# Layer-norm centring moved from ScalarE to VectorE in a strided view, and the score masking moved ahead of the reciprocal

## The chip, the cores and the metric

The kernel runs on one core of a Trainium2 chip. The metric is the time of one execution on the device in microseconds (us), taken as the median of several runs. Lower is better. The engines are TensorE (PE in the profile; PEld is its weight load), VectorE (DVE), ScalarE (ACT), GpSimd (POOL) and SyncE (SP), which issues the DMAs.

## The reference, cut to what matters

One transformer layer over x of 16 batches x 512 tokens x 128 channels, in two parts.

```
mod = (silu(c) @ wmod).reshape(16, 6, 1, 128);  sa, ca, ga, sb, cb, gb = ...
h = layernorm(x) * (1 + ca) + sa                 # centring: (x - mean) / sqrt(var + eps)
x = x + ga * attn(h)                             # rms_norm, q/k/v for 16 heads of 64, rope,
                                                 # softmax in a causal window of 32, w_out
h = layernorm(x) * (1 + cb) + sb
x = x + gb * ffn(h)                              # small attention, layer norm, 8 experts by argmax, layer norm
```

Only the first part, the attention, is touched.

## The kernel before, in words

The attention part is one loop, written out in full, over steps `s` = 0 to 136. There are 16 batches and 8 steps for each (`G = 8`), since a step takes two of the 16 heads; `b, r = s // 8 + 1, s % 8`, so that within a step `r` is the place in the batch and `b` the next batch. Each engine has its own list of instructions, in the order in which the code is written, and semaphores join the lists. Nothing is reordered by a scheduler: an instruction that waits holds everything behind it on its engine.

A pair of heads passes through a pipeline of steps, so that in one step each engine works on several pairs:

- step s: TensorE projects q and k of pair s (lines 323 to 325, three matmuls each for a high/low split), VectorE multiplies them by cos and sin (L503, L504, four instructions, `mm`), SyncE issues four DMAs that swap halves (`sw<-mm`, L222) and three for the values (`vw<-vn`).
- step s+1: GpSimd adds the two halves (L621, `qk`).
- step s+2 (`LS`): TensorE forms the scores (L337). VectorE adds the mask and takes the minimum in eight instructions (L528, `sm` and `mn`), the **masking**.
- step s+3 (`LE`): ScalarE takes the exponential (L692, eight instructions, `pr` and `sums`). VectorE takes the **reciprocal** of the sums (L511, `ri`). GpSimd **normalises** with it (L627, `pr<-pr,ri`).
- step s+4: TensorE transposes `pr` (L352), ScalarE copies it to `pT` (L702). Step s+5: TensorE multiplies by the values (L368), ScalarE and VectorE split the result in a high and a low part (L711 `oth`, L548 `otl`).
- step s+6: TensorE accumulates the output projection of the batch in one PSUM bank, `ACC` (L393, L394, L396). When the eighth pair of a batch is in, VectorE copies `ACC` to `yt` (L518). This is in a step with r = 6. The next batch's first accumulation, also in a step with r = 6, may not start before that copy is done: TensorE waits on `s_yt` ahead of L393.

Beside it the next batch's input is prepared, a little in each step. VectorE takes the statistics of x in a step with r = 3 (`layer_stats`, L412, L417). GpSimd forms 1/sqrt(var + eps) at r = 7 (`shape`, L569, L571, `lnr`) and, for ScalarE's form of the centring, -mean times it (L572, L574, `lnb`). ScalarE **centres** in two halves at r = 0 and r = 1, as its last work of the step (L673, four instructions of 128 x 128 for each batch, `hh`). GpSimd multiplies `hh` by the modulation at r = 1 (L578) and adds at r = 2 (L582), ScalarE squares at r = 3 and 4 (L654), GpSimd finishes the rms norm at r = 4 and 5. At r = 6 TensorE transposes the result (L288), ScalarE copies it (L661, `xh`), and VectorE forms its low part (L428, `xl`, the function `x_low`), for which the q projection of the next step (r = 7) waits, since both use the same PSUM banks in turn.

VectorE's order within a step is: rope (L503, L504), reciprocal, copy of `yt` (r = 6 only), masking, `x_low` (r = 6 only), the gated output (L541, r = 0 only), `otl`, statistics (r = 3 only). The first batch is centred on VectorE ahead of the loop (L422).

Of the kernel before, what the change touches and what calls it, by code (L numbers as in the profile page):

```python
# [10 lines left out]
ALU = mybir.AluOpType  # L11
ACT = mybir.ActivationFunctionType
AX = mybir.AxisListType

P = 128
NB, T, C = 16, 512, 128
NH, G = 16, 8
NI = NB * G
# [8 lines left out]
WK, NW = 96, T // 64  # L27


def program(nc, a, out, debug=None):  # L30
# [7 lines left out]
    with top:  # L38
        def sbt(ctx, name, shape, dt=F32):
            return ctx.enter_context(nc.sbuf_tensor(name, shape, dt))  # L40
# [19 lines left out]
        p1 = ExitStack()  # L60
# [14 lines left out]
        lnr = sbt(p1, "lnr", [P, 4])  # L75
        lnb = sbt(p1, "lnb", [P, 4])
        ssq = sbt(p1, "ssq", [P, 4])
# [53 lines left out]
        s_mk = sem("a_mk")  # L131
# [53 lines left out]
        with nc.Block(no_gpsimd_drain=True) as blk:  # L185
# [214 lines left out]
            def _(dve):  # L400
# [18 lines left out]
                def centre(b):  # L419
                    dve.wait_ge(s_ln, 4 * b + 2)  # L420
                    for j in range(4):
                        ins = dve.tensor_scalar(hh[:, j, :], xt[b % 4][:, j, :], mv[:, j, 0:1], lnr[:, j:j + 1],  # L422
                                                ALU.subtract, ALU.mult)
                    ins.then_inc(s_hc, 1)
# [68 lines left out]
                for s in range(SLOTS):  # L493
                    for j in range(2):
                        if s < NI:
                            u = pj_use[("rope", s, j)]
                            dve.wait_ge(s_pj, u + 1)
                            if s == 0:
                                dve.wait_ge(s_cs, 32)
                            if s >= 2 and j == 0:  # L500
                                dve.wait_ge(s_add, s - 1)
                                dve.wait_ge(s_sw[s % 2], 64 * (s // 2))
                            dve.tensor_tensor(mm[s % 2][:, 0, j, :], PJ[u % 2][:, :], cos[:, :], ALU.mult)  # L503
                            dve.tensor_tensor(mm[s % 2][:, 1, j, :], PJ[u % 2][:, :], sin[:, :], ALU.mult)\  # L504
                                .then_inc(s_rope, 1)
                    i = s - LE
                    if 0 <= i < NI:
# [5 lines left out]
                    if 0 <= i < NI and i % G == G - 1:  # L513
# [4 lines left out]
                        dve.tensor_copy(yt[:, :], ACC[:, :]).then_inc(s_yt, 1)  # L518
                    i = s - LS
                    if 0 <= i < NI:  # L520
                        dve.wait_ge(s_sc, i + 1)
                        if i == 0:
                            dve.wait_ge(s_mk, 3)
                        if i >= 2:
                            dve.wait_ge(s_exp, 2 * i - 2)
                        for h in range(2):
                            for p in range(4):
                                ins = dve.tensor_tensor_reduce(ms_[i % 2][:, h, p, :], SC[h][:, p * WK:(p + 1) * WK],  # L528
                                                               msk[:, min(p, 1), :], 1.0, 3.0e38, ALU.add, ALU.min,
                                                               mn[i % 2][:, h, p:p + 1])  # L530
                            ins.then_inc(s_mx, 1)
                    if s % G == 6 and s // G + 1 < NB:
# [17 lines left out]
                    if s in (2, 3):  # L550
# [3 lines left out]
                                          woh[:, 4 * m:4 * m + 4, :].bitcast(F32), ALU.subtract).then_inc(s_wol, 1)  # L554
                    if s % G == 3 and s // G + 2 < NB:
                        layer_stats(s // G + 2)

            @blk.gpsimd
            def _(pool):
# [4 lines left out]
                def shape(b):  # L564
# [4 lines left out]
                    pool.tensor_scalar(lnr[:, :], mv[:, :, 1], EPS, None, ALU.add).then_inc(s_ln, 1)  # L569
                    pool.wait_ge(s_ln, 4 * b + 1)  # L570
                    pool.tensor_tensor(lnr[:, :], lnr[:, :], nhalf[:, :], ALU.pow).then_inc(s_ln, 1)  # L571
                    pool.tensor_scalar(lnb[:, :], mv[:, :, 0], -1.0, None, ALU.mult).then_inc(s_ln, 1)  # L572
                    pool.wait_ge(s_ln, 4 * b + 3)
                    pool.tensor_tensor(lnb[:, :], lnb[:, :], lnr[:, :], ALU.mult).then_inc(s_ln, 1)  # L574
                    yield
# [72 lines left out]
            def _(act):  # L648
# [16 lines left out]
                for n in range(3):  # L665
                    c = slice(1024 * n, 1024 * n + 1024)
                    act.wait_ge(s_wf[n], 16)
                    act.activation(wh[:, c], wf3[:, c], ACT.Copy, scale=(-0.125, 1.0, 1.0)[n]).then_inc(s_whi, 1)
                def centre(b, k):
                    act.wait_ge(s_ln, 4 * b + 4)  # L670
                    act.wait_ge(s_xn, b)
                    for j in (2 * k, 2 * k + 1):
                        ins = act.activation(hh[:, j, :], xt[b % 4][:, j, :], ACT.Identity, scale=lnr[:, j:j + 1],  # L673
                                             bias=lnb[:, j:j + 1])
                    if k:
                        ins.then_inc(s_hc, 1)

                act.wait_ge(s_rm, 2)
# [4 lines left out]
                for s in range(SLOTS):  # L683
# [33 lines left out]
                    if s < NI:  # L717
# [6 lines left out]
                        act.activation(vn[s % 4][:, :], PJ[u % 2][:, :], ACT.Copy).then_inc(s_ve, 1)  # L724
                    if b < NB and r in (0, 1):
                        centre(b, r)
                    if b < NB and r in (3, 4):
# [860 lines left out]
```

## Time and profile before

| | |
|---|---|
| median of 3 runs | 1189.38 us (1188.65 to 1190.33) |
| the profiled execution's own time | 1190.33 us |
| its span in the trace | 1188.4 us |
| PE busy | 1066.2 us, 90% |
| DVE busy | 940.7 us, 79% |
| ACT busy | 923.1 us, 78% |
| POOL busy | 874.5 us, 74% |
| L673, the centring on ACT, x60 | 26.1 us busy |
| L511, the reciprocal, x128 | 25.2 us busy, 27.0 us idle before it, 26.4 of them for ACT pr |
| L528, the masking, x1024 | 189.8 us busy |

The busy times overlap: all engines work at once, and the shares say nothing yet of which one sets the pace. A row of the timeline gives the start, the length, the engine, the line and what was computed; idle time of the engine just before the row stands in brackets with what ended it. Instructions of one engine overlap by some tens of nanoseconds, so the distance between two starts is the cost of the first, and the length printed is a little more. The attention part lasts until about 775 us; what follows it is not touched.

### The profile page before, as it was taken

How to read it: one execution, taken by the hardware profiler on the slowest of the kernel's cores; microseconds unless marked ns; L12 is line 12 of the kernel's file. 1: busy time of each engine (PE TensorE's matmuls, PEld its weight loads, DVE VectorE, ACT ScalarE, POOL GpSimd, SP SyncE). 2: the span in 40 equal slices, each digit the busy share in tenths (PEclk: the TensorE clock that was granted, in tenths of full speed). 3: DMA queues.
4: the chain of work that ended last, by engine and by line, in shares of the span. 5: the costliest groups of instructions: out<-in, count | busy, mean ns of one | idle time of the engine just before them, and what ended most of it. 6: DMA issues, size and time to landing. Idle time of an engine off the chain costs nothing. (4 is left out here: it accounts for less than half of the span.)

```text
span 1188.4 us, 51662 instructions
## 1 busy us (share of the span) xinstructions
PE 1066.2 (90%) x18513; PEld 863.6 (73%) x18513; DVE 940.7 (79%) x4130; ACT 923.1 (78%) x3404; POOL 874.5 (74%) x732
## 2 busy tenths in 40 slices
PE   4799999999999999999999998847998884499994
PEld 2577877777778777877877886635877774488883
DVE  6988988889889889889888886446887864288885
ACT  2799999999999999999999996736866752266662
POOL 2788888888888888888878875454666767167777
PEclk7999999999999999999999998859998885699997
DMA  6777777776776777777776776262243122666210
GB/s 199 197 183 170 189 180 170 187 182 166 194 178 167 191 177 174 186 178 171 187 177 167 179 180 152 71 196 73 66 140 106 56 81 106 196 194 178 85 33 31
DMA packets 111036, 181.02 MB, mean 152 GB/s; under 512 B 19726, under 2 KB 64177, under 8 KB 110656
## 3 DMA queue, kind: packets, MB, share of 16 engines
q1 hardware_dynamic: 102944, 158.53, 52.5%
q0 software_dynamic: 6400, 16.82, 3.9%
q8 instruction: 152, 2.49, 0.9%
q10 hardware_dynamic: 1440, 2.36, 0.7%
q14 instruction: 100, 0.82, 0.2%
HBM read 35.20 MB, written 24.73 MB: 50 GB/s over the span
## 5 line engine op out<-in xcount | busy, mean ns | idle before, releaser
L621 POOL TENSOR_TENSOR qk<-mm,sw 128x1024 f32<-128x1024 f32 x128 | 305.1, 2384 | 115.3 <-DMA sw<-mm 114.8
L692 ACT ACTIVATE pr<-sm,mn 128x96 f32<-128x96 f32 x1024 | 368.5, 369 | 0.3 <-DVE mn L528 0.3
L503 DVE TENSOR_TENSOR mm<-bank,cos 128x512 f32<-128x512 f32 x256 | 175.1, 684 | 70.9 <-PE bank L325 58.9
L692 ACT ACTIVATION_READ_ACCUMULATOR pr<-sm,mn 128x1 f32 x1024 | 200.8, 196 | 0.0
L627 POOL TENSOR_TENSOR pr<-pr,ri 128x768 f32<-128x768 f32 x128 | 188.8, 1475 | 3.4 <-DVE ri L511 3.4
L528 DVE CUSTOM_DVE_ANT_0 sm<-bank,msk 128x96 f32<-128x96 f32 x1024 | 189.8, 250 | 0.0
L504 DVE TENSOR_TENSOR mm<-bank,sin 128x512 f32<-128x512 f32 x256 | 174.0, 680 | 0.0
L368 PE MATMUL bank<-pT,vw 96*64 96x64 f32 x4096 | 150.3, 227 | 0.0
L702 ACT ACTIVATE pT<-bank 96x512 f32<-96x512 f32 x256 | 137.0, 585 | 17.1 <-PE bank L352 15.3
L368 PEld LDWEIGHTS bank<-pT,vw 96*64 96x64 f32 x4096 | 132.5, 140 | 10.4 <-issue 0.7
L337 PEld LDWEIGHTS bank<-qk 64*64 64x64 f32 x4096 | 90.7, 133 | 55.9 <-issue 54.4
L337 PE MATMUL bank<-qk 64*64 64x96 f32 x4096 | 114.7, 250 | 9.3 <-POOL qk L621 9.3
L1295 ACT ACTIVATE fv<-bank,b1t 128x128 f32<-128x128 f32 x288 | 82.4, 369 | 52.1 <-PE bank L1156 51.9
L323 PE MATMUL bank<-xh,wh 128*128 128x512 f32 x256 | 104.9, 410 | 3.3 <-DVE xl L428 1.4
L724 ACT ACTIVATE vn<-bank 128x512 f32<-128x512 f32 x128 | 76.2, 596 | 37.4 <-PE bank L301 37.3
L325 PE MATMUL bank<-xh,wl 128*128 128x512 f32 x256 | 102.4, 400 | 0.0
L324 PE MATMUL bank<-xl,wh 128*128 128x512 f32 x256 | 101.9, 398 | 0.0
L1002 POOL DMA_INDIRECT out<-h,rr x72 | 76.7, 1065 | 30.5 <-issue 27.0
L548 DVE TENSOR_TENSOR otl<-bank,oth 128x512 fp32r<-128x512 f32 x128 | 87.7, 685 | 8.4 <-ACT oth L711 8.4
L352 PE MATMUL bank<-ident,pr 64*96 64x64 f32 x2048 | 84.0, 222 | 6.2 <-POOL pr L627 5.9
L997 POOL DMA_INDIRECT sorted_scratch<-rr,slot x64 | 65.6, 1025 | 29.2 <-issue 17.9
L528 DVE DVE_READ_ACCUMULATOR2_ANT mn<- 128x1 f32 x1024 | 84.5, 83 | 0.1
(210 smaller groups left out, 2476.8 us busy)
## 6 DMA issues: line engine op xcount, KB each, us to landing
sw<-mm SPq DMA_DIRECT2D x512, 128.0 KB, 2.4
vw<-vn SPq DMA_DIRECT2D x128, 192.0 KB, 2.6
vw<-vn SPq DMA_DIRECT2D x128, 128.0 KB, 2.4
rr<-sorted_scratch SPq DMA_DIRECT2D x72, 192.5 KB, 2.7
vw<-vn SPq DMA_DIRECT2D x96, 64.0 KB, 2.2
xt<-in_x SPq DMA_DIRECT2D x16, 256.0 KB, 4.5
x_scratch<-x SPq DMA_DIRECT2D x16, 256.0 KB, 2.7
rr<-x_scratch SPq DMA_DIRECT2D x16, 256.0 KB, 2.9
```

The source lines that it names most:

```text
L323: pe.matmul(dst[:, :], wh[:, o:o + P], xh[b % 2][:, :], start=True, stop=False)
L324: pe.matmul(dst[:, :], wh[:, o:o + P], xl[b % 2][:, :], start=False, stop=False)
L325: pe.matmul(dst[:, :], wl[:, o:o + P], xh[b % 2][:, :], start=False, stop=True).then_inc(s_pj, 1)
L337: ins = pe.matmul(SC[h][64 * e:64 * e + 64, p * WK:(p + 1) * WK], t[r, 0, 32 + 64 * w:96 + 64 * w], t[r, 1, 64 * w:64 * w + WK], start=Tru ...
L368: ins = pe.matmul(OB[64 * h:64 * h + 64, 64 * w:64 * w + 64], vw[half % 2][:, w, c:c + 64], pT[i % 2][:, h, 64 * w:64 * w + 64], start=Tru ...
L503: dve.tensor_tensor(mm[s % 2][:, 0, j, :], PJ[u % 2][:, :], cos[:, :], ALU.mult)
L504: dve.tensor_tensor(mm[s % 2][:, 1, j, :], PJ[u % 2][:, :], sin[:, :], ALU.mult)\
L528: ins = dve.tensor_tensor_reduce(ms_[i % 2][:, h, p, :], SC[h][:, p * WK:(p + 1) * WK], msk[:, min(p, 1), :], 1.0, 3.0e38, ALU.add, ALU.mi ...
L621: pool.tensor_tensor(qk[i % 2][:, :, 32:], mm[i % 2][:, 0, :, :], sw[i % 2][:, :, :], ALU.add)\
L627: pool.tensor_tensor(t, t, ri[i % 2][:, :].unsqueeze(2).to_broadcast([P, 8, WK]), ALU.mult)\
L692: ins = act.activation(pr[i % 2][:, h, p, :], ms_[i % 2][:, h, p, :], ACT.Exp, scale=-1.0, bias=mn[i % 2][:, h, p:p + 1], accum_out=sums[i ...
L702: act.activation(pT[i % 2][:, :, :].rearrange("k h (p e q) -> k (h p) e q", p=4, e=2)[:, :, e, :], TR[e][0:WK, :].rearrange("k (a q) -> k ...
```

## The change: what it does

1. The centring of batches 1 to 15 leaves ScalarE and enters VectorE's list at r = 1, behind `otl`, all four instructions in one step. It waits for `lnr`, and for the previous batch's `xn`.
2. The centring on VectorE, the first batch's too, reads and writes its 128 elements in the order 0, 2, 4, ..., 126, 1, 3, ..., 127: a view of 2 x 64 with a step of 2 elements inside.
3. GpSimd no longer forms `lnb` (two instructions for each batch), and the counts of its semaphore are adjusted.
4. In VectorE's list the masking of pair s-2 now comes straight behind the rope, ahead of the reciprocal of pair s-3 and of the copy of `yt`.

```diff
@@ centre, now for all batches @@
-                    dve.wait_ge(s_ln, 4 * b + 2)
+                    dve.wait_ge(s_ln, 2 * b + 2)
+                    if b:
+                        dve.wait_ge(s_xn, b)
                     for j in range(4):
-                        ins = dve.tensor_scalar(hh[:, j, :], xt[b % 4][:, j, :], mv[:, j, 0:1], lnr[:, j:j + 1],
-                                                ALU.subtract, ALU.mult)
+                        o, x = (v.rearrange("p (a k) -> p k a", k=2) for v in (hh[:, j, :], xt[b % 4][:, j, :]))
+                        ins = dve.tensor_scalar(o, x, mv[:, j, 0:1], lnr[:, j:j + 1], ALU.subtract, ALU.mult)
                     ins.then_inc(s_hc, 1)
@@ VectorE's loop: the masking block moves up unchanged, from behind the yt copy @@
+                    i = s - LS
+                    if 0 <= i < NI:
+                        dve.wait_ge(s_sc, i + 1)
...
+                            ins.then_inc(s_mx, 1)
                     i = s - LE
                     if 0 <= i < NI:
                         dve.wait_ge(s_exp, 2 * i + 2)
@@ end of VectorE's loop @@
-                    if s % G == 3 and s // G + 2 < NB:
-                        layer_stats(s // G + 2)
+                    b, r = s // G + 1, s % G
+                    if b < NB:
+                        if r == 1:
+                            centre(b)
+                    if r == 3 and b + 1 < NB:
+                        layer_stats(b + 1)
@@ GpSimd, shape @@
-                    pool.tensor_scalar(lnb[:, :], mv[:, :, 0], -1.0, None, ALU.mult).then_inc(s_ln, 1)
-                    pool.wait_ge(s_ln, 4 * b + 3)
-                    pool.tensor_tensor(lnb[:, :], lnb[:, :], lnr[:, :], ALU.mult).then_inc(s_ln, 1)
@@ ScalarE @@
-                def centre(b, k):
-                    act.wait_ge(s_ln, 4 * b + 4)
-                    act.wait_ge(s_xn, b)
-                    for j in (2 * k, 2 * k + 1):
-                        ins = act.activation(hh[:, j, :], xt[b % 4][:, j, :], ACT.Identity, scale=lnr[:, j:j + 1],
-                                             bias=lnb[:, j:j + 1])
-                    if k:
-                        ins.then_inc(s_hc, 1)
...
-                    if b < NB and r in (0, 1):
-                        centre(b, r)
```

VectorE's list in a step with r = 6, before; L528 is the masking (each instruction has a second row for its minimum), and the names in brackets are the semaphores waited for:

```order
L504 TENSOR_TENSOR mm<-bank,sin 128x512
L511 RECIPROCAL ri<-sums 128x8 [waits a_nm,a_exp]
L518 COPY yt<-bank 128x512 [waits a_pj,a_op]
L528 ISA sm,mn<-bank,msk 128x96 [waits a_exp,a_sc]
L528 ISA mn 128x1
...
L428 TENSOR_TENSOR xl<-bank,xh 128x512 [waits a_xh]
```

And the same step now, where the lines have moved (L516 is the masking, L525 the reciprocal, L532 the copy of `yt`, L429 the low part of x):

```order
L505 TENSOR_TENSOR mm<-bank,sin 128x512
L516 ISA sm,mn<-bank,msk 128x96 [waits a_exp,a_sc]
L516 ISA mn 128x1
...
L525 RECIPROCAL ri<-sums 128x8 [waits a_nm,a_exp]
L532 COPY yt<-bank 128x512 [waits a_pj,a_op]
L429 TENSOR_TENSOR xl<-bank,xh 128x512 [waits a_xh]
```

The eight masking instructions now stand between the last rope instruction and both the reciprocal and the copy; the low part of x has the same instructions ahead of it as before.

VectorE's list at the end of a step with r = 1 now, the next step's rope behind it; before, L548 (`otl`) was followed at once by the rope:

```order
L525 RECIPROCAL ri<-sums 128x8 [waits a_nm,a_exp]
L549 TENSOR_TENSOR otl<-bank,oth 128x512 [waits a_op,a_ot]
L424 TENSOR_SCALAR hh<-xt,mv,lnr 128x2x64 [waits a_xn,a_ln]
L424 TENSOR_SCALAR hh<-xt,mv,lnr 128x2x64 x3
L504 TENSOR_TENSOR mm<-bank,cos 128x512 [waits a_sw0,a_add,a_pj]
```

Four instructions (L424) have come in ahead of the next step's rope.

## Rows read from the trace of the kernel before

**Rows 1.** By stretch: length, busy PE, PEld, DVE, ACT, POOL; clock, DMA share, GB/s.
```profile
70.00:704.00 634.00, 630.40 (x10449) 504.93 (x10446) 561.41 (x2629) 601.92 (x2429) 536.12 (x365) 1.00 0.72 178
```

**Rows 2.** Waits over the whole run: us in total, times, longest.
```profile
DVE ri L511 <- ACT pr L692: 26.4, 56, 3.0
...
PEld bank L323 <- DVE xl L428: 9.8, 16, 1.8
```

**Rows 3.** Timeline of DVE, step 70 (r = 6): start, length, engine, line.
```profile
415.90 0.69 DVE L503 TENSOR_TENSOR mm<-bank,cos 128x512 f32<-128x512 f32 x1 [0.35 <-PE bank L325]
...
418.31 0.19 DVE L511 RECIPROCAL ri<-sums 128x8 f32<-128x8 f32 x1
418.42 0.64 DVE L518 COPY yt<-bank 128x512 f32<-128x512 f32 x1
...
420.39 0.68 DVE L428 TENSOR_TENSOR xl<-bank,xh 128x512 fp32r<-128x512 f32 x1
```

**Rows 4.** Timeline of PE at the same place, steps 70 and 71.
```profile
420.17 0.39 PE L393 MATMUL bank<-oth,woh 128*128 128x512 f32 x1
420.40 0.39 PE L394 MATMUL bank<-oth,wol 128*128 128x512 f32 x1
...
421.13 0.50 PE L323 MATMUL bank<-xh,wh 128*128 128x512 f32 x1
421.47 0.39 PE L324 MATMUL bank<-xl,wh 128*128 128x512 f32 x1
```

**Rows 5.** Timeline of PE and DVE, step 126 (the last with r = 6).
```profile
743.02 0.39 PE L393 MATMUL bank<-oth,woh 128*128 128x512 f32 x1
...
741.54 0.19 DVE L511 RECIPROCAL ri<-sums 128x8 f32<-128x8 f32 x1
```

**Rows 6.** Timeline of ACT at the end of the loop (steps 127, 128).
```profile
748.68 0.60 ACT L724 ACTIVATE vn<-bank 128x512 f32<-128x512 f32 x1 [0.28 <-PE bank L301]
749.17 0.37 ACT L692 ACTIVATE pr<-sm,mn 128x96 f32<-128x96 f32 x1
```

**Rows 7.** Timeline of DVE, step 65 (r = 1) into step 66.
```profile
391.20 0.20 DVE L511 RECIPROCAL ri<-sums 128x8 f32<-128x8 f32 x1 [0.39 <-ACT pr L692]
391.32 0.26 DVE L528 CUSTOM_DVE_ANT_0 sm<-bank,msk 128x96 f32<-128x96 f32 x1
...
392.75 0.69 DVE L548 TENSOR_TENSOR otl<-bank,oth 128x512 fp32r<-128x512 f32 x1
393.79 0.69 DVE L503 TENSOR_TENSOR mm<-bank,cos 128x512 f32<-128x512 f32 x1 [0.36 <-PE bank L325]
```

**Rows 8.** Timeline of POOL, steps 65 and 66.
```profile
392.02 1.48 POOL L627 TENSOR_TENSOR pr<-pr,ri 128x768 f32<-128x768 f32 x1
394.00 1.28 POOL L578 TENSOR_TENSOR hh<-hh,mod 128x512 f32<-128x512 f32 x1 [0.50 <-ACT hh L673]
397.01 2.42 POOL L621 TENSOR_TENSOR qk<-mm,sw 128x1024 f32<-128x1024 f32 x1 [1.73 <-DMA sw<-mm]
399.38 1.48 POOL L627 TENSOR_TENSOR pr<-pr,ri 128x768 f32<-128x768 f32 x1
```

**Rows 9.** Timeline of PE, step 67 (r = 3).
```profile
400.91 0.65 PE L352 MATMUL bank<-ident,pr 64*96 64x64 f32 x16 [0.18 <-POOL pr L627]
```

**Rows 10.** Timeline of DVE and POOL, step 2.
```profile
35.08 2.10 DVE L553 TENSOR_TENSOR wol<-x,woh 128x512 fp32r<-128x512 f32 x1
...
34.26 2.38 POOL L621 TENSOR_TENSOR qk<-mm,sw 128x1024 f32<-128x1024 f32 x1 [1.86 <-DMA sw<-mm]
```

**Rows 11.** The line of the first batch's centring: ns min/median/max, first and last start.
```profile
L422 DVE TENSOR_SCALAR hh<-xt,mv,lnr x4: 345/346/348, 6.5 to 7.3; 128x128 f32<-128x128 f32 x4
```

**Rows 12.** Timeline of POOL, steps 7 to 8 (first batch), and PE behind it.
```profile
70.41 0.23 POOL L572 TENSOR_SCALAR lnb<-mv 128x4 f32<-128x4 f32 x1
...
70.88 2.41 POOL L621 TENSOR_TENSOR qk<-mm,sw 128x1024 f32<-128x1024 f32 x1
...
74.77 0.65 PE L352 MATMUL bank<-ident,pr 64*96 64x64 f32 x16 [0.29 <-POOL pr L627]
```

More of the change, by code:

```diff
@@ L75, in program @@
         lnr = sbt(p1, "lnr", [P, 4])
-        lnb = sbt(p1, "lnb", [P, 4])
         ssq = sbt(p1, "ssq", [P, 4])
@@ L505, in _ @@
                                 .then_inc(s_rope, 1)
+                    i = s - LS
+                    if 0 <= i < NI:
+                        dve.wait_ge(s_sc, i + 1)
+                        if i == 0:
+                            dve.wait_ge(s_mk, 3)
+                        if i >= 2:
+                            dve.wait_ge(s_exp, 2 * i - 2)
+                        for h in range(2):
+                            for p in range(4):
+                                ins = dve.tensor_tensor_reduce(ms_[i % 2][:, h, p, :], SC[h][:, p * WK:(p + 1) * WK],
+                                                               msk[:, min(p, 1), :], 1.0, 3.0e38, ALU.add, ALU.min,
+                                                               mn[i % 2][:, h, p:p + 1])
+                            ins.then_inc(s_mx, 1)
                     i = s - LE
@@ L518, in _ @@
                         dve.tensor_copy(yt[:, :], ACC[:, :]).then_inc(s_yt, 1)
[L519 to L531, printed above, removed]
                     if s % G == 6 and s // G + 1 < NB:
@@ L569, in shape @@
                     pool.tensor_scalar(lnr[:, :], mv[:, :, 1], EPS, None, ALU.add).then_inc(s_ln, 1)
-                    pool.wait_ge(s_ln, 4 * b + 1)
+                    pool.wait_ge(s_ln, 2 * b + 1)
                     pool.tensor_tensor(lnr[:, :], lnr[:, :], nhalf[:, :], ALU.pow).then_inc(s_ln, 1)
-                    pool.tensor_scalar(lnb[:, :], mv[:, :, 0], -1.0, None, ALU.mult).then_inc(s_ln, 1)
-                    pool.wait_ge(s_ln, 4 * b + 3)
-                    pool.tensor_tensor(lnb[:, :], lnb[:, :], lnr[:, :], ALU.mult).then_inc(s_ln, 1)
                     yield
```

## The prediction, on record before the changed kernel was run

> **What bounds the kernel now.** I read the busy time by stretch first. From 70 to 704 us TensorE is busy 630.4 of 634 us at full granted clock [rows 1]. ScalarE with 601.9 and VectorE with 561.4 are nearly full beside it, but not full. TensorE is one nearly unbroken row of matmuls, 3.6 us of idle in 634. So in this stretch a change pays or costs only where TensorE waits. Second I read the waits. VectorE's reciprocal waits 26.4 us in total for ScalarE [rows 2], which looks large, but it is idle time of an engine that TensorE paces: the rope behind it waits for TensorE in every step shown [rows 3, 7]. TensorE's own repeated wait is one at r = 7, where L323 waits for `xl`: 9.8 us over 16 batches as its weight load sees it [rows 2]. Third I read the timeline around each place where the change moves something, and asked which TensorE instruction waits for it and how much room it has.
>
> **The order on VectorE, r = 6: the copy of `yt`.** Eight masking instructions take 392.75 - 391.32 = 1.43 us [rows 7]. They now stand ahead of the reciprocal (0.11 us to the next start) and the copy. The copy therefore starts at 418.31 + 1.43 + 0.11 = 419.85 instead of 418.42 [rows 3]. L393 of the next batch waits for its end. How long after its start can TensorE go on? The low part of x, as long (0.68 against 0.64), starts at 420.39 and TensorE starts at 421.13, 0.74 later [rows 3, 4]; less 0.04 for the shorter instruction that is 0.70. So L393 starts at about 420.55 instead of 420.17 [rows 4]: a new wait of 0.38 us. But TensorE was about to wait there anyway. Before, L393, L394 and L396 were done in time and L323 then waited until 421.13. Now they run at 420.55, 420.89 (the first matmul after a wait is followed after 0.34 us, 421.47 - 421.13, and not after 0.23, 420.40 - 420.17 [rows 4]) and 421.12, and L323 comes at 421.35. `xl` itself is not later, since the same instructions stand ahead of it and their sum is the same. L324 comes at 421.58 instead of 421.47: 0.11 us for each batch. There are 15 steps with r = 6 at which a copy and a waiting L393 meet, s = 14 to 126. For 14 of them this holds: 14 x 0.11 = 1.5 us. The last one, s = 126, has no next batch and no `xl` to hide behind. There the copy would start at 741.54 + 1.54 = 743.08 and L393 at 743.78 instead of 743.02 [rows 5], with 0.11 for the restart: 0.87 us. Does the end of the loop hide it? ScalarE takes pair 125's exponentials at 749.17 straight behind the values of step 127, which wait for TensorE [rows 6], with no idle between. If ScalarE or anything later had slack there, it would cost 0; I find no such slack in these rows and count it in full. Sum of this edit: 2.4 us slower.
>
> **The order on VectorE, every step: the masking earlier, the reciprocal later.** The masking no longer stands behind the wait of 0.39 us [rows 7], so it gains 0.4 to 0.5 us in such steps. No TensorE wait for it is worth a row, so nothing comes of it in time. The reciprocal is 1.43 us later where it did not wait, about 1.0 us where it did. It releases the normalising on GpSimd (L627). Where GpSimd comes to it later anyway, as at 399.38 behind the addition that waited 1.73 us for a DMA [rows 8], nothing is lost. At r = 1 it moves from 392.02 to about 390.73 (rope ended) + 1.43 + 0.28 = 392.4, with the transposes three microseconds off. I take 0 here, except as in the next part.
>
> **The centring on VectorE, r = 1.** ScalarE loses 26.1 us of work (the table), VectorE gains 60 instructions. The contiguous form takes 345 ns each and starts every 0.26 us ((7.3 - 6.5)/3) [rows 11]; the strided form is not in the trace. Lower bound 4 x 0.26 = 1.0 us for a batch, upper bound 4 x 0.346 = 1.4 us, as if nothing overlapped; I take 1.0, nearest to the row. Can GpSimd hold it up? L553, an instruction of VectorE on two SBUF operands, took 2.10 us against 0.69 for `otl` of the same size, and ended half a microsecond after GpSimd's L621 ended (34.26 + 2.38 = 36.64) [rows 7, 10]: it waited out the whole GpSimd instruction. The centring has one tensor operand. If it waits in the same way, it stands behind the normalising, which now runs from 392.4 to 393.9; if not, it starts at 392.9 behind `otl`. So the rope of step 66 starts at 393.9 + 1.0 = 394.9 or at 393.9, against 393.79 [rows 7]: 0.1 to 1.1 us later, and with the upper bound of the centring up to 1.5. The Trainium skill, in "SBUF — State Buffer", section "Who interferes with whom", says that tensor_scalar in a two-port mode takes the pair of ports that VectorE shares with GpSimd, for the whole instruction. In "VectorE: DVE Perf Modes", section "Mode 2×_2P", it makes that mode depend on an even outermost dimension, which the 2 of the new view is as well. By that rule the later start, 394.9, holds in either view; I take it.
>
> Who waits for that rope? The next reciprocal no longer waits in front of the masking, so half of the delay is taken back. Masking starts at 394.9 + 2.41 = 397.3 (four rope instructions, 418.31 - 415.90 [rows 3]) and the reciprocal at 398.7. Normalising is possible from 399.0. GpSimd was at it at 399.38 in this batch, where the addition waits for its DMA; in batches whose DMA is earlier the new bound is 399.0, end 400.5. TensorE's transposes would come at 400.91 - 0.18 = 400.73 [rows 9]. So 0.2 us of room is left. Behind the rope stand the step's DMAs on SP and the addition of step 67 on GpSimd, which itself stands behind the 1.3 us of L582 (as long as L578 [rows 8]), so it could start no earlier than 399.38 + 1.48 + 1.28 = 402.1. The step's four DMAs have from 397.3 until then, 4.8 us; the step before's took from about 391 to 397.01 with a transfer queued ahead. If they should need as much, the addition is 1 us late, and the room of the transposes behind it decides; I count 0. The multiplication L578 starts at 395.1 instead of 394.0 and ends at 396.4, ahead of 397.01 [rows 8]. Cost 0; if the room is missed, see B.
>
> **GpSimd without `lnb`, r = 7.** 0.47 us less for a batch (70.88 - 70.41) [rows 12]. In a steady batch the next addition waits for its DMA and nothing comes of it. In the first batch the addition follows at once and TensorE waits 0.29 us for what follows: 0.3 us faster, once. ScalarE's freed time, 26.1 us, lies off TensorE's path: 0. The startup (steps 0 to 3) is paced by the DMA queue (the addition there waits 1.86 us for it [rows 10]), and a late centring there costs at most 1 us, by its 4 x 0.26; I take 0.
>
> **The sum**, on the profiled execution's 1190.33 us (span 1188.4): + 1.5 + 0.9 - 0.3 = + 2.1, so 1192.4. The profiled execution is the slowest of the three; their median is 0.95 lower, so 1191.5 us for the median.
>
> **Rivals.** A is the sum above. **B, slower:** the normalising misses the transposes at r = 3. It decides from the 0.2 us of room: with a strided centring of 0.346 us each, 0.35 more, TensorE waits 0.15 in each of 15 batches; with half a microsecond more lost at the hand-over it waits 0.65. That is 2 to 10 us on top of A; I price it at 5: 1196.5. For it speaks that such a wait is there already in some batches [rows 9], against it that the late ones come from the DMA and would hide the centring. **C, faster:** ScalarE was the true pace, since its 601.9 of 634 us leave little room [rows 1]. Then up to 26.1 us come back: 1163, or 1189.4 - 26.1/2 = 1176 if every second batch gains. Against it: the row of matmuls has no gap for ScalarE to have made. **D, no change:** the waits for `yt` are taken up by the loop's other slack (an earlier DMA against the later TensorE), 1189.4.
>
> **Numbers.** A 0.58, B 0.15, C 0.07, D 0.20. A measurement of this kernel can tell about 0.2%, 2.4 us, so slower begins at 1191.8. A's own range is 1190.2 to 1193; four tenths of it lie beyond 1191.8. Slower: 0.24 + 0.15 = 0.39. Faster: 0.07 + 0.02 of D = 0.09. Same: 0.52. The range for eight in ten takes in D and most of B: 1188.6 to 1197.
>
> **What would show it.** PE L393 waits at r = 6, 0.3 to 0.4 us, for the copy of `yt`, and the `xl` wait of the next matmul is gone or short. At s = 126 that wait is 0.75 us. The rope of a step with r = 2 starts up to 1.1 us later and the reciprocal's wait for ScalarE is nearly gone from the list, with the time unmoved. The centring's first instruction is longer than the other three if GpSimd holds it. ScalarE is 26 us less busy. The prediction is wrong if TensorE's steps with r = 1 to 3 grow (B), or if steps that had no wait become shorter (C).

## The result, and the profile after

The changed kernel takes 1195.54 us (median of 20 runs, 1189.73 to 1203.61) beside 1189.09 us of the kernel before on the same chip (20 runs, 1179.77 to 1194.13). The ratio is 1.006, 95% interval 1.0043 to 1.0078: slower by 0.4 to 0.8%. The predicted 1191.5 us had the direction of case A, to which the prediction gave 0.58, but by its own limit of 0.2% it held "same" for likelier (0.52) than "slower" (0.39). The measured time lies in its range, near the upper end, and the addition of 6.5 us is three times the 2.1 us that the sum gave. Each ratio in this text is worked out from the fast runs of both kernels, so it is not always the quotient of the two medians beside it.

The profiled execution took 1199.29 us with a span of 1197.4. That is 3.8 us above the median of its kernel, and the profiled execution of before is 1.2 above its own, so the two traces lie 9.0 us apart and the medians 6.5. The attention stretch first: length, busy PE, PEld, DVE, ACT, POOL; clock, DMA share, GB/s.

```profile
70.00:704.00 634.00, 623.83 (x10323) 498.29 (x10323) 575.22 (x2650) 583.83 (x2347) 525.17 (x332) 1.00 0.70 176
```

TensorE was busy 630.4 us in this stretch [rows 1] and is busy 623.8 now, and 126 fewer of its matmuls fall into it. ScalarE is busy 18 us less and VectorE 14 us more, at the same granted clock (over the whole run ScalarE fell by 12 us, from 923.1 to 910.9, where the prediction said 26). Freed time on ScalarE bought nothing. What TensorE lost can be read from its waits in the same stretch, of the kernel after (total us, times, longest):

```profile
PE bank L392 <- DVE yt L532: 4.0, 14, 0.3
PE bank L351 <- POOL pr L629: 3.8, 10, 0.4
PE bank L336 <- POOL qk L623: 2.3, 5, 1.2
```

And of the kernel before:

```profile
PE bank L352 <- POOL pr L627: 1.5, 5, 0.4
PE bank L337 <- POOL qk L621: 0.5, 1, 0.5
```

The wait for the copy of `yt` is new. The waits for GpSimd, for the normalising and for the addition, were there and have grown from 2.0 us in 6 places to 6.1 in 15. I measured each step as the distance from the first value matmul of the step before to its own (L299 before, L298 after). From step 8 to step 120 the sum went from 631.3 to 639.5 us. Of these 8.2 us, 14 steps with r = 7 hold 2.2 (5.82 to 5.98 each), 14 with r = 3 hold 2.4 (5.64 to 5.81), 14 with r = 4 hold 2.7 (5.47 to 5.66); the rest is scattered. The step s = 127 adds 0.9, and step 8 is reached 0.8 us earlier.

**The copy of `yt`.** PE and DVE at r = 6, step 70, of the kernel after:

```profile
424.31 0.64 DVE L532 COPY yt<-bank 128x512 f32<-128x512 f32 x1
425.09 0.47 PE L392 MATMUL bank<-oth,woh 128*128 128x512 f32 x1 [0.29 <-DVE yt L532]
425.40 0.39 PE L393 MATMUL bank<-oth,wol 128*128 128x512 f32 x1
425.63 0.40 PE L395 MATMUL bank<-otl,woh 128*128 128x512 f32 x1
425.87 0.40 PE L322 MATMUL bank<-xh,wh 128*128 128x512 f32 x1
426.10 0.39 PE L323 MATMUL bank<-xl,wh 128*128 128x512 f32 x1
```

The wait sits where the prediction put it, and L322 follows L395 after 0.24 us with no wait for `xl` any more. L392 starts 0.78 us behind the start of the copy (the prediction took 0.70). At the last such step, s = 126:

```profile
750.55 0.64 DVE L532 COPY yt<-bank 128x512 f32<-128x512 f32 x1
751.34 0.47 PE L392 MATMUL bank<-oth,woh 128*128 128x512 f32 x1 [0.67 <-DVE yt L532]
```

The same matmul started at 743.02 [rows 5], so 8.3 us are gathered by here, of the 9.0 by which the two spans differ.

**The centring.** DVE from step 17 (r = 1) into step 18, of the kernel after:

```profile
122.34 1.93 DVE L424 TENSOR_SCALAR hh<-xt,mv,lnr 128x128 f32<-128x128 f32 x4
124.19 0.68 DVE L504 TENSOR_TENSOR mm<-bank,cos 128x512 f32<-128x512 f32 x1
```

Four instructions of 0.34 us, which start every 0.26, would be over in 1.1 us. They take 1.93. GpSimd in the same kernel at the same time, and on into step 19:

```profile
121.95 1.47 POOL L629 TENSOR_TENSOR pr<-pr,ri 128x768 f32<-128x768 f32 x1 [0.69 <-DVE ri L525]
124.42 1.28 POOL L580 TENSOR_TENSOR hh<-hh,mod 128x512 f32<-128x512 f32 x1 [1.00 <-DVE hh L424]
126.11 2.41 POOL L623 TENSOR_TENSOR qk<-mm,sw 128x1024 f32<-128x1024 f32 x1 [0.42 <-DMA sw<-mm]
...
132.64 2.41 POOL L623 TENSOR_TENSOR qk<-mm,sw 128x1024 f32<-128x1024 f32 x1 [1.45 <-DMA sw<-mm]
```

The normalise, released by the late reciprocal, runs from 121.95 to 123.42, and the first centring instruction, 1.16 us long by itself, is over 0.08 us behind it. So it is in 14 of the 15 batches: the first centring instruction ends 0.08 or 0.09 us behind a GpSimd instruction that was running. The rope L504 starts at 124.19, straight behind the centring. Before, the rope waited for TensorE instead:

```profile
123.30 0.39 PE L325 MATMUL bank<-xh,wl 128*128 128x512 f32 x1
123.73 0.69 DVE L503 TENSOR_TENSOR mm<-bank,cos 128x512 f32<-128x512 f32 x1 [0.35 <-PE bank L325]
```

The same matmul in the kernel after:

```profile
122.91 0.40 PE L324 MATMUL bank<-xh,wl 128*128 128x512 f32 x1
```

So the rope is 1.28 us behind its matmul and not 0.43: 0.85 us late, and 0.93 on average over the 14 steps with r = 2 from 9 to 119 (measured from the first value matmul of the step before). The rope's DMAs are late with it, by 0.81 us on average. DMA issues of SP in this place, of the kernel after:

```profile
126.69 2.65 SPq L221 DMA_DIRECT2D sw<-mm  x4
```

and of the kernel before, with the addition that followed:

```profile
126.24 2.65 SPq L222 DMA_DIRECT2D sw<-mm  x4
...
131.27 2.40 POOL L621 TENSOR_TENSOR qk<-mm,sw 128x1024 f32<-128x1024 f32 x1
```

Before, the addition came 5.0 us behind the start of the issues and did not wait for them. After, it came 5.95 us behind and waited 1.45. So the DMAs were issued late and were also slow here. TensorE, at step 20 (r = 4), of the kernel after:

```profile
135.20 0.89 PE L336 MATMUL bank<-qk 64*64 64x96 f32 x32 [0.24 <-POOL qk L623]
136.54 0.65 PE L351 MATMUL bank<-ident,pr 64*96 64x64 f32 x16 [0.45 <-POOL pr L629]
```

The transposes' wait (L351) has the same cause: their normalising (L629) starts straight behind the late addition. So it is in all ten of L351's waits in this stretch: the normalising starts straight behind an addition that had waited for its DMA, and never behind the late reciprocal.

**Which of these waits can come from the late rope.** The rope that stands behind the centring is that of a step with r = 2. Its addition is in the next step and its scores are in the one after, r = 4. So through its own DMAs and addition the late rope reaches TensorE at r = 4, not at r = 3. Of the 6.1 us of waits for GpSimd, 2.1 are at r = 4, where before had none, and 3.8 at r = 3, where before had 1.7 of its 2.0 (the rest stands at other steps). The waits at r = 3 stand behind DMAs of the steps with r = 1, which are issued ahead of the centring. The longest of all is one of them, in steps 65 to 67 of the kernel after:

```profile
391.19 0.69 DVE L504 TENSOR_TENSOR mm<-bank,cos 128x512 f32<-128x512 f32 x1 [0.70 <-PE bank L324]
394.82 2.42 SPq L221 DMA_DIRECT2D sw<-mm  x4
395.68 2.26 DVE L424 TENSOR_SCALAR hh<-xt,mv,lnr 128x128 f32<-128x128 f32 x4
401.46 2.39 POOL L623 TENSOR_TENSOR qk<-mm,sw 128x1024 f32<-128x1024 f32 x1 [2.11 <-DMA sw<-mm]
404.00 0.89 PE L336 MATMUL bank<-qk 64*64 64x96 f32 x32 [1.18 <-POOL qk L623]
```

The rope is over and the four issues are under way before the centring starts, and the addition still waits for them, until 6.6 us behind the first issue. From the first of the four issues to the last landing it took, at r = 1, 4.3 to 6.1 us in the trace of before and 4.3 to 6.6 in that of after; at r = 2 it took 4.1 to 5.6 and 4.1 to 5.9.

**The late reciprocal.** GpSimd's wait for it, from the page of the kernel after, in the columns busy, mean ns, idle before and releaser:

```profile
L629 POOL TENSOR_TENSOR pr<-pr,ri 128x768 f32<-128x768 f32 x128 | 188.6, 1473 | 35.1 <-DVE ri L525 34.2
```

and of the kernel before:

```profile
L627 POOL TENSOR_TENSOR pr<-pr,ri 128x768 f32<-128x768 f32 x128 | 188.8, 1475 | 3.4 <-DVE ri L511 3.4
```

The 26.4 us of VectorE's wait for ScalarE [rows 2] are gone from the page, and GpSimd has 31 us of new idle time in their place. The experiments ask which of these is paid for.

### The profile page after: what moved, and what is told of

It is laid out like the page before. It is cut to its first block and busy times, and to the rows that moved or that the text cites. A ratio compares the mean times of both kernels' runs of the same rounds, so it can differ in the third digit from the quotient of the medians.

```text
span 1197.4 us, 51615 instructions
## 1 busy us (share of the span) xinstructions
PE 1067.7 (89%) x18513; PEld 863.6 (72%) x18513; DVE 963.9 (81%) x4190; ACT 910.9 (76%) x3344; POOL 869.2 (73%) x700
## 5 line engine op out<-in xcount | busy, mean ns | idle before, releaser
L504 DVE TENSOR_TENSOR mm<-bank,cos 128x512 f32<-128x512 f32 x256 | 175.1, 684 | 72.8 <-PE bank L324 62.1
L629 POOL TENSOR_TENSOR pr<-pr,ri 128x768 f32<-128x768 f32 x128 | 188.6, 1473 | 35.1 <-DVE ri L525 34.2
L685 ACT ACTIVATION_READ_ACCUMULATOR pr<-sm,mn 128x1 f32 x1024 | 195.9, 191 | 0.0
L516 DVE CUSTOM_DVE_ANT_0 sm<-bank,msk 128x96 f32<-128x96 f32 x1024 | 191.0, 252 | 3.0 <-PE bank L336 3.0
L322 PE MATMUL bank<-xh,wh 128*128 128x512 f32 x256 | 103.5, 404 | 2.7 <-DVE xl L429 1.4
L323 PE MATMUL bank<-xl,wh 128*128 128x512 f32 x256 | 102.1, 399 | 0.0
L549 DVE TENSOR_TENSOR otl<-bank,oth 128x512 fp32r<-128x512 f32 x128 | 84.7, 662 | 14.6 <-ACT oth L704 14.0
L351 PE MATMUL bank<-ident,pr 64*96 64x64 f32 x2048 | 85.0, 224 | 5.7 <-POOL pr L629 5.5
L516 DVE DVE_READ_ACCUMULATOR2_ANT mn<- 128x1 f32 x1024 | 84.6, 83 | 0.0
```

What stands on the lines that cost most here:

```text
L322: pe.matmul(dst[:, :], wh[:, o:o + P], xh[b % 2][:, :], start=True, stop=False)
L323: pe.matmul(dst[:, :], wh[:, o:o + P], xl[b % 2][:, :], start=False, stop=False)
L629: pool.tensor_tensor(t, t, ri[i % 2][:, :].unsqueeze(2).to_broadcast([P, 8, WK]), ALU.mult)\
L685: ins = act.activation(pr[i % 2][:, h, p, :], ms_[i % 2][:, h, p, :], ACT.Exp, scale=-1.0, bias=mn[i % 2][:, h, p:p + 1], accum_out=sums[i ...
```

## The experiments

Twelve runs were made, in three groups of four; each group shared one chip and its own runs of the kernel before. Theory 1 has two costs: the wait for `yt`, and the rope with r = 2 that is late behind the centring. Rival 2 is the order alone, rival 3 the centring alone. The first chip is a slower one for this kernel (before: 1234.09 us, 35 runs, 1219.78 to 1246.04); only ratios, and the waits and steps of the attention part, are compared across chips.

### First group: each part alone

**Order only**: the kernel before, with nothing but the masking moved.

```diff
-    reciprocal(i = s-3);  copy yt;  masking(i = s-2)
+    masking(i = s-2);  reciprocal(i = s-3);  copy yt
```

> The kernel before with one edit: the masking stands ahead of the reciprocal and of the copy of yt in VectorE's list; the centring stays on ScalarE. Theory 1 (two costs: the wait for yt at r = 6, and a late rope at r = 2 behind the centring): only the first is here, 14 x 0.17 us and 0.94 us once, as the steps of the changed kernel's trace grew, so 3.3 us slower, ratio 1.003; TensorE waits for the copy of yt in 15 steps, and no more often than before for the addition or the normalising. Rival 2 (the order alone is the cause): the full 6 to 7 us, ratio 1.006. Rival 3 (the centring alone is the cause, the yt wait is taken up elsewhere): 1.000.

Measured 1235.27 us, ratio 1.0024 (0.9985 to 1.0064). Its trace has the waits for `yt`, and steps with r = 7 of 5.98 us. Steps 8 to 120 take 634.0 us against 631.3. The interval holds 1.003 and 1.006, so the time doesn't decide between theory 1 and rival 2. From 70 to 704 us (total us, times, longest):

```profile
PE bank L393 <- DVE yt L531: 4.1, 14, 0.3
PE bank L352 <- POOL pr L627: 2.2, 6, 0.4
PE bank L337 <- POOL qk L621: 0.2, 1, 0.2
```

**Centring only**: the changed kernel with the old order.

```diff
-    masking(i = s-2);  reciprocal(i = s-3);  copy yt
+    reciprocal(i = s-3);  copy yt;  masking(i = s-2)
```

> The changed kernel with the old order (reciprocal, copy of yt, masking): only the centring has moved to VectorE and lnb is gone. Theory 1: 3 to 4.5 us slower than before, ratio 1.003 to 1.004; no wait for yt, the four centring instructions take about 1.9 us together in a step, TensorE waits at r = 3 and r = 4 for the addition and the normalising in about half of the batches. Since the reciprocal still waits for ScalarE ahead of the masking here, the late rope is not made up for, and it may be up to 1 us a batch worse. Rival 2: 1.000. Rival 3: 1.006.

Measured 1230.06 us, ratio 0.9994 (0.9951 to 1.0037). No wait for `yt`, and 1.9 us of waits for GpSimd from 70 to 704 us, no more than before. This is below the 1.003 to 1.004 that theory 1 gave, though the interval just reaches it. The centring waits less, since the normalise is released earlier and ends earlier (in step 17 it starts 1.0 us ahead of the centring, in the kernel after 0.4). DVE's L424 from 80 to 740 us in this kernel (busy us, mean ns):

```profile
L424 DVE TENSOR_SCALAR hh<-xt,mv,lnr 128x128 f32<-128x128 f32 x52 | 20.4, 454 | 0.0
```

and in the kernel after, where the two parts of the change meet:

```profile
L424 DVE TENSOR_SCALAR hh<-xt,mv,lnr 128x128 f32<-128x128 f32 x52 | 25.6, 552 | 0.0
```

The other three instructions being 0.34 us each, the first one takes 4 x 0.552 - 3 x 0.339 = 1.19 us with the new order and 4 x 0.454 - 3 x 0.341 = 0.79 with the old.

**Contiguous view**: the changed kernel with the centring in plain order.

```diff
-    o, x = (v.rearrange("p (a k) -> p k a", k=2) for v in (hh[:, j, :], xt[b % 4][:, j, :]))
-    ins = dve.tensor_scalar(o, x, mv[:, j, 0:1], lnr[:, j:j + 1], ALU.subtract, ALU.mult)
+    ins = dve.tensor_scalar(hh[:, j, :], xt[b % 4][:, j, :], mv[:, j, 0:1], lnr[:, j:j + 1],
+                            ALU.subtract, ALU.mult)
```

> The changed kernel with the centring's view made contiguous again (128 elements in a row instead of 2 x 64 with a step of 2). Theory 1 with the shared ports held in either view: nothing changes, ratio to before 1.006 as for the changed kernel, the four instructions take 1.9 us together as there. Rival (the strided view avoids a lock that the contiguous one takes): GpSimd's or VectorE's waits grow, 1.008 or more. Rival (the strided access costs time by itself): the last three instructions get shorter than 0.26 us apart and the ratio falls to 1.004.

Measured 1236.88 us, ratio 1.0043 (1.0004 to 1.0082). At the place shown above (step 17), in this kernel:

```profile
122.19 1.93 DVE L423 TENSOR_SCALAR hh<-xt,mv,lnr 128x128 f32<-128x128 f32 x4
```

The view makes no difference, to 0.01 us: it waits out the normalise in either. In all 15 batches the first instruction ends 0.08 or 0.09 us behind a GpSimd instruction.

**`yt` first**: the changed kernel with the copy ahead of the masking.

```diff
-    masking(i = s-2);  reciprocal(i = s-3);  copy yt
+    copy yt;  masking(i = s-2);  reciprocal(i = s-3)
```

> The changed kernel with the copy of yt put ahead of the masking (order: yt copy, masking, reciprocal). Theory 1: the wait for yt goes, 3.3 us back, ratio to before 1.003; the waits at r = 3 and r = 4 stay. Rival 2 (order alone): the masking still stands ahead of the reciprocal, so 1.006 if it is the late reciprocal, 1.000 if it is the yt copy. Rival 3 (centring alone): 1.006.

Measured 1238.52 us, ratio 1.0067 (1.0028 to 1.0105). The waits for `yt` are gone and steps with r = 7 are back at 5.82 us, but the time is not lower than that of the other kernels of this group. Steps 8 to 120 take 635.1 us. I take from it that the wait for `yt` is likely not the whole cost; how large the rest is, this group can't say, with intervals of 0.8%.

### Second group: without the wait of the centring

**The changed kernel again.**

> The changed kernel once more, as the measure for the three others on this chip. Both theories: 1.006 of the kernel before, in the trace 15 waits of the output projection for the copy of yt, steps with r = 7 at 5.98 us, and steps 8 to 120 about 8 us longer in sum than before (639.5 against 631.3).

Measured 1200.11 us (7 runs, 1198.37 to 1207.72) beside 1191.07 of before: 1.0092 (1.0056 to 1.0127). Steps 8 to 120: 639.3 us, 0.1 from the first trace.

**Another form of the centring**, in plain order as in the third kernel, which also writes a sum.

```diff
-    o, x = (v.rearrange("p (a k) -> p k a", k=2) for v in (hh[:, j, :], xt[b % 4][:, j, :]))
-    ins = dve.tensor_scalar(o, x, mv[:, j, 0:1], lnr[:, j:j + 1], ALU.subtract, ALU.mult)
+    ins = dve.tensor_scalar(hh[:, j, :], xt[b % 4][:, j, :], mv[:, j, 0:1], lnr[:, j:j + 1],
+                            ALU.subtract, ALU.mult, accum_out=cj[:, j:j + 1])
```

> The changed kernel, but the centring is contiguous and also writes a sum that nobody reads (accum_out), another form of the same instruction. Theory 1 (the centring delays the next rope because its first instruction waits out GpSimd's normalise): if this form does not wait, the four take about 1.1 to 1.4 us and not 1.93, the rope with r = 2 comes 0.6 to 0.8 us earlier, the waits of TensorE for the addition and the normalise at r = 3 shrink, steps 8 to 120 fall from 639.5 to about 636, time 2 to 4 us below the changed kernel. The 15 waits for yt stay. If the first instruction is 1.1 us here too, the lock belongs to every form and the time stays. Rival 2 (the order alone costs, the centring nothing): the time stays in either case.

Measured 1196.19 us, ratio 1.005 (1.0026 to 1.0074). DVE at step 17 in this kernel:

```profile
122.84 0.40 DVE L424 TENSOR_SCALAR_CACHE_REDUCE hh<-xt,mv,lnr 128x128 f32<-128x128 f32 x1
123.16 0.08 DVE L424 DVE_READ_ACCUMULATOR hh<-xt,mv,lnr 128x1 f32 x1
123.16 0.40 DVE L424 TENSOR_SCALAR_CACHE_REDUCE hh<-xt,mv,lnr 128x128 f32<-128x128 f32 x1
...
124.14 0.69 DVE L505 TENSOR_TENSOR mm<-bank,cos 128x512 f32<-128x512 f32 x1
```

and GpSimd at the same time:

```profile
122.44 1.47 POOL L630 TENSOR_TENSOR pr<-pr,ri 128x768 f32<-128x768 f32 x1 [0.15 <-DVE ri L526]
```

The normalise runs until 123.91, and the centring starts in the middle of it and is not held: 1.30 us from the first start to the rope, though each instruction is longer. Steps 8 to 120 fall to 636.6 us, 2.7 to 2.9 under the two traces of the changed kernel. In all 15 batches each of the four instructions takes 0.40 us. The time is 4 us lower, as expected; the two intervals overlap, so the time alone doesn't prove it. The closest pair speaks against it: the contiguous view of the first group, which differs by the added sum alone and is held, had 1.0043 and steps 8 to 120 of 636.9 us on its chip, about as much as this kernel.

**Order without the wait for `yt`**: the kernel before, in the order of the fourth kernel, the centring on ScalarE.

> The kernel before, with the order at r = 6 and elsewhere rope, copy of yt, masking, reciprocal; the centring stays on ScalarE. Theory 1: no wait for yt, no centring on VectorE, so only the late reciprocal is left: steps 8 to 120 within 1.5 us of before (631.3), 1.000 to 1.001. Rival 2 (the reciprocal behind the masking costs by itself): steps with r = 3 to 4 longer by 0.1 us each and the time 2 to 4 us above before, 1.002 to 1.003.

Measured 1190.53 us, ratio 1.0001 (0.9974 to 1.0028). GpSimd waits for the late reciprocal as much as in the changed kernel:

```profile
POOL pr L627 <- DVE ri L531: 32.3, 52, 2.8
```

and it costs nothing that can be measured in the time. The trace missed what theory 1 expected: steps 8 to 120 take 633.8 us, 2.5 above before and not within 1.5. The steps with r = 3 and 4 are 0.06 and 0.07 us longer, and TensorE waits 3.6 us for GpSimd where it waited 2.0, each time behind an addition that waited for its DMA.

**An attempt at less than both**: the kernel before, with TensorE's transposes of `xn` earlier.

```diff
+    if r == 6: to_columns(b)           # ahead of the multiplication by the values
     ... pT x vw ...
-    if r == 6: to_columns(b)
@@ VectorE, r = 6 @@
-    masking h=0;  masking h=1;  x_low
+    masking h=0;  x_low;  masking h=1
```

> The kernel before with another edit, a try at less than both: at r = 6 TensorE transposes xn ahead of the multiplication by the values (line 368) instead of behind it, and VectorE forms xl between the two halves of the masking. TensorE's wait for xl ahead of the first matmul of r = 7 (0.27 us of idle, 15 times) goes: steps with r = 7 5.82 to about 5.55, time about 4 us less, 0.9965. If ScalarE's copy xh comes too late for VectorE, the second half of the masking and the exponential behind it are late, and the gain is half or none.

Measured 1191.04 us, ratio 0.9998 (0.9971 to 1.0025): no gain. TensorE at step 70 in this kernel:

```profile
417.58 0.66 PE L288 MATMUL bank<-ident,xn 128*128 128x128 f32 x4
418.17 1.15 PE L370 MATMUL bank<-pT,vw 96*64 96x64 f32 x32
...
420.51 0.39 PE L396 MATMUL bank<-otl,woh 128*128 128x512 f32 x1
420.74 0.40 PE L323 MATMUL bank<-xh,wh 128*128 128x512 f32 x1
```

Before, L396 stood at the same place with 0.50 us to L323 (421.13 [rows 4]):

```profile
420.63 0.40 PE L396 MATMUL bank<-otl,woh 128*128 128x512 f32 x1
```

The wait for `xl` is gone (0.23 from L396 to L323 now). But L288 now costs 0.59 us to the next start, where it cost 0.41 ahead of the value projection (its L299). Taken from the first matmul of a step (L323) to that of the next, the step with r = 6 went from 6.13 to 6.05 us and the one behind it from 5.56 to 5.47. That is 0.17 for a batch and 15 x 0.17 = 2.6 us in all, more than half undone in this trace by three batches that were longer, and less than the measurement can tell.

### Third group: the parts again, and both costs taken away

> The kernel before with the new order on VectorE alone, once more, since the first measure had an interval of 0.8%. Theory 1 (wait for yt 3.3 us, and a late rope behind a centring that waits out the normalise): 15 waits for yt, ratio 1.002 to 1.004. Rival 2 (the order is all of it): 1.006.

Order only: 1196.71 us beside 1191.75, ratio 1.0049 (1.0024 to 1.0074). 15 waits for `yt`, 4.8 us. This is above the range of theory 1, and the interval holds rival 2's 1.006. Steps 8 to 120 take 638.0 us, 6.7 above before and only 1.5 under the kernel after, and TensorE waits 6.1 us for GpSimd from 70 to 704 us, as much as there, though the centring is on ScalarE. The wait at step 20 that was shown for the kernel after is here too, and longer:

```profile
127.65 2.67 SPq L222 DMA_DIRECT2D sw<-mm  x4
136.74 0.89 PE L337 MATMUL bank<-qk 64*64 64x96 f32 x32 [0.74 <-POOL qk L621]
```

The last of these four transfers landed 6.5 us behind the first issue, in the kernel after 5.9, in the trace of before 4.8.

> The changed kernel with the old order on VectorE (reciprocal, yt, masking), once more. Theory 1, sharpened: the normalise is released early and is nearly over when the centring comes, so the first centring instruction waits for less of it (mean of all four 0.45 us and not 0.55, as the first such run showed). Ratio 1.000 to 1.003. Rival 3 (the centring on VectorE is all of it): 1.006.

Centring only: 1193.95 us, ratio 1.0024 (0.9999 to 1.0049). L424 averages 438 ns. But this trace has steps with r = 3 of 5.90 us and, from 70 to 704 us,

```profile
PE bank L351 <- POOL pr L629: 4.1, 11, 0.4
PE bank L336 <- POOL qk L623: 2.9, 6, 0.9
```

7.0 us of waits for GpSimd where the first trace of the same kernel had 1.9. Steps 8 to 120 take 638.6 us here and 633.3 there. So these stalls differ by as much between two executions, on two chips, as I had wanted to explain.

**`yt` first, and the form that is not held**: the edits of the fourth and the sixth kernel together.

> The changed kernel with the copy of yt ahead of the masking, and with the form of the centring that does not wait for GpSimd (accum_out). Theory 1: both costs are gone, what stays is 1.3 us of centring for a batch in VectorE's room: steps 8 to 120 about 633 to 634, 1.001 to 1.003, under the changed kernel by 5 to 7 us. Rival: a cost that neither names, 1.005 or more.

Measured 1192.62 us, ratio 1.0008 (0.9985 to 1.0032). This is the change whole, centring on VectorE and masking early, with both costs of theory 1 taken away, and it is level with before. Steps 8 to 120 take 634.6 us.

**Old order, and the form that is not held**: the edit of the sixth kernel in the second one.

> The changed kernel with the old order and with the form that does not wait: the mildest way to move the centring. Theory 1: 0.999 to 1.002, that is no gain either, since TensorE sets the pace and ScalarE's freed 26 us are worth nothing. If ScalarE had been a second pace beside TensorE, it is 4 us or more below before.

Measured 1192.11 us, ratio 0.9997 (0.9971 to 1.0024). No gain either. No kernel that ran beats the one before.

## Why the prediction was right, and where it was not

- **The number: in the range, partly by luck.** The sum gave 1191.5 us. The measured 1195.54 is within a microsecond of case B (1196.5, chance 0.15), which the range took in. By the prediction's own sign ("wrong if TensorE's steps with r = 1 to 3 grow") the sum of case A failed, since the steps with r = 3 grew by 0.17 us each. About half of the added time, 3.2 of 6.5 us, is the cost that the sum names.
- **What bounds the stage: right.** TensorE sets the pace. ScalarE lost the centring in seven kernels that are level with before or slower, and case C (ScalarE as the pace) is out.
- **The wait for `yt`: shown in the traces.** It appears with the order alone and goes with the order alone (steps with r = 7 of 5.98 us in every kernel that has the wait, of 5.82 or 5.83 in every one without, the edited transposes apart). The ratios agree (1.0024 and 1.0049 with it, 1.0001 without), but their intervals overlap. The term was mis-sized: 0.11 us for a batch predicted, 0.16 measured. The copy's start to L392 was put at 0.70, taken from the low part of x, and is 0.78; those 0.08 pass to L323 in full, less the 0.03 by which the matmul after a wait followed sooner (0.31 for 0.34). At s = 126 it was 0.94 for 0.87. In all 14 x 0.16 + 0.94 = 3.2 us for 2.4.
- **The late reciprocal at no cost: right by the time.** 32 us of waiting on GpSimd in the seventh kernel, ratio 1.0001 (0.9974 to 1.0028). Its trace was 2.5 us longer in the steps 8 to 120, so a cost of a microsecond or two isn't excluded.
- **The hold of the centring: right.** The rule from the Trainium skill that the prediction took its later start from, in "SBUF — State Buffer", section "Who interferes with whom", agrees with this trace in both views (1.93 us for the four in either). The rope with r = 2 is 0.85 us late in the place shown and 0.93 on average (predicted 1.1 for step 66).
- **"I count 0" for what stands behind that rope: the term that was missing.** The prediction asked whether the four DMAs would need as much as the 4.8 us they had, and took it that they would not. In the trace of before they had landed 4.1 to 5.6 us behind the first issue, mean 4.6, so for the slower ones there was no room. With the issue 0.8 us later TensorE waited at r = 4, for the addition and for the transposes behind it: 2.1 us in the first trace, 1.1 in the second, none before. But order only has such waits too (0.5 and 1.2) without the centring on VectorE, and of what grew at r = 3 and 4 (5.1 us in the first trace and 4.6 in the second) 2.4 and 3.2 us are at r = 3, ahead of the place that the late rope reaches. Case B named the transposes at r = 3 as well, but behind a late normalising; here the normalising followed its addition at once, and the addition was late behind its DMA. Case B had held it against itself that "the late ones come from the DMA", and that is what the traces show.
- **What is shown, and what is not.** The order's wait for `yt` accounts for 3.2 us. For the other 3 us no cause is shown. Theory 1 puts them on a centring that is held behind a late reciprocal. For it speaks that `yt` first with the centring on VectorE had 1.0067, with the centring on ScalarE 1.0001 and with the form that is not held 1.0008; the three ran on different chips and the intervals touch (1.0028 to 1.0105, 0.9974 to 1.0028, 0.9985 to 1.0032). Taking the hold away took 4 us off the changed kernel (1.0092 to 1.005), but beside the first measure, 1.006 with 20 runs and the narrowest interval, it took off little, and beside the contiguous view (1.0043) nothing. Rival 2, order alone, is not excluded: its 1.0049 (1.0024 to 1.0074) holds 1.006, and its second trace has the steps and the waits of the kernel after to 1.5 us. Rival 3, centring alone, asked for 1.006 and is out as the whole cost: 0.9994 (0.9951 to 1.0037) and 1.0024 (0.9999 to 1.0049). The single traces don't size the second cost either, as the table shows. Waits for GpSimd of 4.4 to 5.2 us stand in four kernels of which three are level with before. The only trace of before, with 2.0, may be a quiet one, since its steps 8 to 120 are shorter than those of every other kernel, the level ones too (632.4 to 635.1). How much of the rest is the late issue, how much the order by itself and how much slow DMAs stays open; several traces of each kernel on one chip would be needed.

| kernel | ratio | steps 8 to 120 | TensorE's waits for GpSimd, 70 to 704 us | of them at r = 4 | for `yt` |
|---|---|---|---|---|---|
| before | 1 | 631.3 | 2.0 | 0 | 0 |
| after, two traces | 1.006, 1.0092 | 639.5, 639.3 | 6.1, 5.9 | 2.1, 1.1 | 4.0, 4.0 |
| order only, two | 1.0024, 1.0049 | 634.0, 638.0 | 2.4, 6.1 | 0.5, 1.2 | 4.1, 4.1 |
| centring only, two | 0.9994, 1.0024 | 633.3, 638.6 | 1.9, 7.0 | 0.4, 1.5 | 0 |
| contiguous view | 1.0043 | 636.9 | 3.6 | 1.1 | 4.0 |
| `yt` first | 1.0067 | 635.1 | 3.4 | 1.1 | 0 |
| form that is not held | 1.005 | 636.6 | 4.7 | 1.0 | 4.1 |
| same, `yt` first | 1.0008 | 634.6 | 5.1 | 0 | 0 |
| same, old order | 0.9997 | 635.1 | 5.2 | 0 | 0 |
| order, no wait for `yt` | 1.0001 | 633.8 | 3.6 | 1.0 | 0 |
| earlier transposes of `xn` | 0.9998 | 632.4 | 4.4 | 0 | 0 |

- **The first batch: not shown.** The prediction said 0.3 us, at a wait of TensorE in step 9. The 0.8 us of the first trace are there at step 8, ahead of that place, and the four traces of edited kernels that still form `lnb` reach step 8 early too, at 69.4 to 70.4 us (before 70.6, after 69.8). That the sign agrees is luck as far as these traces go. The wait in step 9 is gone in both traces of the kernel after, but it is there in four other traces without `lnb`.

## What to carry to other kernels

An instruction is cheap or dear by who waits behind it: the late reciprocal made GpSimd idle for 32 us at no cost, and the late copy of `yt` made TensorE wait 0.3 us in each batch, of which half was paid. When work is moved to an engine with room, look at what the other engines are doing at that moment (here a GpSimd instruction held the moved work for a microsecond), and then follow the delay through the DMAs to the next consumer on the critical engine. Count the steps: a delay at r = 2 could reach TensorE at r = 4, and the waits at r = 3 had to have another source. Room behind a DMA is to be taken from its slow cases: the four transfers here had landed 4.1 to 6.8 us behind the first issue in the traces of before and after. Stalls that stand behind DMAs varied by 5 us between two traces of one kernel (1.9 and 7.0), nearly as much as the whole change cost, so one trace finds the mechanism but not its size, and a wait counts as an effect of the edit only when it is missing from kernels without the edit.

## What the runs showed of the hardware that was not expected

- tensor_scalar on VectorE did not end until a running GpSimd tensor_tensor had ended, in a contiguous and in a strided view alike (1.93 us for four in both; 0.08 or 0.09 us behind GpSimd's end in 29 of 30 batches of the two kernels). The same arithmetic with accum_out was not held. It takes 0.40 us and a read of 0.08 where the plain form takes 0.34.
- Four 128 x 128 transposes cost TensorE 0.41 us ahead of the value projection's matmuls and 0.56 to 0.59 ahead of the 64-column ones.
- The kernel before took 1189 to 1192 us in three of the four measurements and 1234 in the other, on another chip. From 70 to 780 us TensorE is busy 692.5 and 690.3 us in the traces of before on the first and of order only on the slow chip. The difference lies behind it: from 790 to 1185 us 6596 matmuls fall into the stretch in the one, 6249 in the other. From the values of step 127 to the end of the span, 477 to 489 us pass in the four traces of the slow chip and 441 to 444 in the ten others. Why stays open.
